# Last cross round rebuilt, the outer loop written out, and the low context made by adding transfers

## The reference

```python
x = _layernorm(x + attn(x))           # 4 "time" rows by 16 heads, and a dynamic convolution
x = _layernorm(x + xattn(x, ctx))     # this one:
    q  = (x @ w_q).reshape(b, n, 16, 64)
    kv = (context @ w_kv).reshape(b, 1601, 2, 16, 64)
    attn = softmax(einsum('bnhd,bmhd->bhnm', q, k) * 64 ** -0.5)
    out  = einsum('bhnm,bmhd->bnhd', attn, v) @ w_out + b_out
x = _layernorm(x + ffn(x))            # softmax over 8 gates, top 2, relu(x W1 + b1) W2 + b2
```

## Time and profile before

| | us |
|---|---|
| median of 3 runs | 1937.08 |
| lowest and highest | 1935.52, 1938.04 |
| profiled execution, its own time | 1938.37 |
| its span, first to last instruction | 1936.6 |

### The profile page before, as it was taken

One profiled execution on the slowest core, in us unless ns is written; L12 is line 12 of the kernel. 1 busy time (PEld: TensorE's weight loads), 2 busy tenths in 40 slices (PEclk: granted clock), 3 DMA queues, 4 the chain that ended last, 5 costly groups with the idle time before them and its releaser, 6 DMA issues. The chain is left out here.

```text
span 1936.6 us, 32752 instructions
## 1 busy us (share of the span) xinstructions
PE 1732.8 (89%) x10604; PEld 1207.0 (62%) x10604; DVE 1178.2 (61%) x2073; ACT 826.8 (43%) x1198; POOL 1277.1 (66%) x709
## 2 busy tenths in 40 slices
PE   6654699999989999998999999989999999847992
PEld 4543566666756666665666666757666665436991
DVE  4776455656565656666665556565656667666665
ACT  3223244444444444444544444444444445421223
POOL 3878248667686676776768577686776776933554
PEclk8776789999999999999999999999999999957996
DMA  6001300000200000010000000100000000241224
GB/s 196 1 22 33 120 1 23 1 23 0 78 1 23 1 24 15 9 56 23 23 1 23 2 23 0 63 16 23 1 23 15 8 16 12 84 145 49 75 77 144
DMA packets 39141, 71.24 MB, mean 37 GB/s; under 512 B 4632, under 2 KB 28568, under 8 KB 37728
## 3 DMA queue, kind: packets, MB, share of 16 engines
q1 hardware_dynamic: 35264, 59.27, 9.1%
q0 software_dynamic: 3744, 10.23, 1.7%
HBM read 55.97 MB, written 13.52 MB: 36 GB/s over the span
## 5 line engine op out<-in xcount | busy, mean ns | idle before, releaser
L1173 POOL TENSOR_TENSOR xa_total<-xa_total,xa_pexp 128x1024 f32<-128x1024 f32 (+1 forms) x341 | 832.4, 2441 | 59.7 <-ACT xa_pexp L1096 35.6
L1271 DVE TENSOR_REDUCE xa_parts<-ps_ring 128x1 f32<-128x402 f32 x1024 | 531.6, 565 | 268.5 <-PE ps_ring L1016 255.4
L1096 ACT ACTIVATE xa_pexp<-ps_s 128x1024 f32<-128x1024 f32 (+1 forms) x416 | 426.2, 1026 | 387.3 <-PE ps_s L970 349.6
L984 PE MATMUL ps_pv<-xa_pexp,xa_v 128*64 128x512 f32 (+1 forms) x1664 | 402.3, 607 | 0.0
L984 PEld LDWEIGHTS ps_pv<-xa_pexp,xa_v 128*64 128x64 f32 (+1 forms) x1664 | 106.7, 137 | 182.0 <-issue 141.6
L970 PE MATMUL ps_s<-xa_q_neg,xa_row_one 64*128 64x512 f32 (+1 forms) x832 | 180.8, 393 | 0.0
L1173 POOL TENSOR_TENSOR xa_total<-xa_pexp 128x1024 f32<-128x1024 f32 x31 | 74.0, 2386 | 159.8 <-ACT xa_pexp L1096 158.5
L1149 ACT COPY xa_v<-ps_ring 128x256 f32<-128x256 f32 (+1 forms) x208 | 77.5, 373 | 204.0 <-PE ps_ring L955 202.2
L1016 PE MATMUL ps_ring<-xa_k_hi,xa_q_hi 64*128 64x402 f32 x512 | 128.7, 378 | 7.8 <-DVE xa_parts L1271 6.9
L1016 PE MATMUL ps_ring<-first_k_hi,xa_q_hi 64*128 64x402 f32 x512 | 122.7, 386 | 3.3 <-DVE xa_q_lo L1265 1.5
L1326 DVE RECIPROCAL xa_inv<-xa_sums 128x128 f32<-128x128 f32 x124 | 116.9, 943 | 0.0
(11 more groups left out here) (303 smaller groups left out, 3376.9 us busy)
## 6 DMA issues: line engine op xcount, KB each, us to landing
wa_raw<-in_pack_a SPq DMA_DIRECT2D x17, 768.0 KB, 4.4
ex_raw<-in_pack_e SPq DMA_DIRECT2D x8, 1024.0 KB, 5.9
ctx_raw<-in_ctxT SPq DMA_DIRECT2D x4, 1601.0 KB, 8.8
wb_raw<-in_pack_b SPq DMA_DIRECT2D x16, 256.0 KB, 2.6
ex_w<-ybuf SPq DMA_DIRECT2D x8, 512.0 KB, 7.4
sa_xT<-in_xT SPq DMA_DIRECT2D x8, 256.0 KB, 6.3
X<-in_x SPq DMA_DIRECT2D x1, 2048.0 KB, 11.7
x_hi<-sa_x1s_hi SPq DMA_DIRECT2D x16, 128.0 KB, 2.1
```

Source lines behind the costliest of these rows:

```text
L984: ins = nc.tensor.matmul(ps_pv[half(h), :], v[0:m, t, at:at + XD], pexp[0:m, buf, h, :], start=t == 0, stop=t == MT - 1)
L1096: nc.scalar.activation(pexp[0:m, buf], ps_s[0:m, (p * MT + t) % 2], ACT.Exp, scale=XD ** -0.5)\
L1173: engine.tensor_tensor(total[p][0:m], first, pexp[0:m, buf], ALU.add).then_inc(s["add_done"], 1)
L1271: nc.vector.tensor_reduce(parts[:, h, q, c:c + 1], ps_ring[:, r, 0:CW], AX.X, ALU.max)\
```

## The change

- The loop over b is written out (three copies of its body); the loops over j stay.
- In a round that ends a batch, ScalarE copies the context halves behind tiles 4 and 6 (they were behind 5 and 8), and behind each copy (tiles 5 and 7) scales the high part by -1 into `ctx_lo` (CN). GpSimd then issues a transfer that adds `ctx_raw` to it. The subtractions of GpSimd and VectorE are gone.
- In the last round WX is split: ScalarE makes the high part, GpSimd the low one. Experts 1, 2 and 0, in that order, are made (the first two in the first half, tiles 3 and 5), expert 3 is left to the expert stage. In the first half the additions of tiles 9 to 12 are VectorE's. Two input buffers changed places in memory, so that the places of experts 1 and 2 are free early.
- In the expert stage experts 3, 4 and 5 have their low parts from GpSimd (5 behind the first gathers), the copy of 7 comes behind the fourth block, and the 32 comparisons of 128 elements are 4 of 1024 in float32.

```diff
@@ one_round
     if batch_ends:
-        loads = join(loads, {0: ([], [("LDC",)]), 2: ([], [("X1",)]), 5: ([], [("CX", 0)]), 8: ([], [("CX", 1)])})
+        loads = join(loads, {0: ([], [("LDC",)]), 2: ([], [("X1",)]), 4: ([], [("CX", 0)]), 5: ([], [("CN", 0)]), 6: ([], [("CX", 1)]), 7: ([], [("CN", 1)])})
...
-        loads = join(loads, {2 * b: ([], [("ST", b)]) for b in range(B - 1)})
+        loads = join(loads, {2 * b: ([], [("ST", b)]) for b in range(B - 1)}, {3: ([], [("WX", 0)]), 5: ([], [("WX", 1)])})
...
-        head = {0: ([], [("WX", 0)]), 1: ([], [("TX", 0), ("WX", 1)]), 3: ([], [("GT", 0), ("TX", 1)]), 5: ([], [("GT", 1), ("TX", 2)]),
-                6: ([], [("WX", 2)]), 7: ([], [("GT", 2), ("TX", 3), ("WX", 3)]), 9: ([], [("GT", 3), ("TX", 4)]),
+        head = {1: ([], [("TX", 0), ("WX", 2)]), 3: ([], [("GT", 0), ("TX", 1)]), 5: ([], [("GT", 1), ("TX", 2)]),
+                7: ([], [("GT", 2), ("TX", 3)]), 9: ([], [("GT", 3), ("TX", 4)]),
@@ walk
-    with eng.Fori(0, B - 1) as b:
+    for b in range(B - 1):
@@ Ahead
-EARLY = 4
+ORDER = (1, 2, 0, 3, 4, 5, 6, 7)
+EARLY = 3
@@ scalar, cross
+                elif kind == "WX":
+                    pos = st[1]
+                    act.wait_ge(ahead.raw_in[pos % STG], 16 * (pos // STG + 1))
...
+                    nc.scalar.copy(ahead.w_all[:, ORDER[pos], 0], ahead.raw[pos % STG][:]).then_inc(ah["w_hi_done"], 1)
...
+                elif kind == "CN":
+                    k = st[1]
+                    act.wait_ge(s["ctx_hi_done"], n.of("CX"))
+                    nc.scalar.mul(ctx_lo[:, k], ctx_hi[:, k].bitcast(F32), -1.0).then_inc(s["ctx_neg"], 1)
@@ additions
-        def adds_on_vector(i, p):
-
-            return isinstance(i, int) and i == QUADS * B - 1 and p == 1
+        def adds_on_vector(i, p, t):
+
+            return isinstance(i, int) and i == QUADS * B - 1 and (p == 1 or t >= 9)
@@ gpsimd, cross
-                elif kind == "CX" and st[1] == 0:
+                elif kind == "CN":
+
                     k = st[1]
-                    pool.wait_ge(s["ctx_hi_done"], n.of("CX") + 1)
-                    nc.gpsimd.tensor_tensor(ctx_lo[:, k], ctx_raw[:, k], ctx_hi[:, k].bitcast(F32), ALU.subtract)\
-                        .then_inc(s["ctx_lo_done"], 1)
+                    pool.wait_ge(s["ctx_neg"], n.of("CN") + 1)
+                    nc.gpsimd.dma_start(ctx_lo[:, k].bitcast(F32), ctx_raw[:, k], accum_op=ALU.add).then_inc(s["ctx_lo_done"], 16)
@@ vector, cross
-                elif kind == "CX" and st[1] == 1:
-
-                    dve.wait_ge(s["ctx_hi_done"], n.of("CX") + 1)
-                    nc.vector.tensor_tensor(ctx_lo[:, 1], ctx_raw[:, 1], ctx_hi[:, 1].bitcast(F32), ALU.subtract)\
-                        .then_inc(s["ctx_lo_done"], 1)
@@ experts
-            take_weights(6)
-            take_weights(7)
+            take_weights(5)
+            take_weights(6)
...
+                if q == 3:
+                    take_weights(7)
...
-                for k in range(n, n + 8):
-                    ins = nc.vector.tensor_scalar(one_r[:, k % 16], iota_h[:], rem[:, k:k + 1], None, ALU.is_equal)
-                ins.then_inc(s["one_r_done"], 1)
+                nc.vector.tensor_tensor(one_r[:, n % 16:n % 16 + 8], iota[:].unsqueeze(1).broadcast_to([P, 8, P]),
+                                        rem[:, n:n + 8].unsqueeze(2).broadcast_to([P, 8, P]), ALU.is_equal)\
+                    .then_inc(s["one_r_done"], 1)
```

More of the change, by code:

```diff
@@ L825, in start @@
         sp.dma_start(self.b1c[:], a["pack_e"][:, :, WW:].rearrange("e p c -> p e c")).then_inc(self.sems["small_in"], 16)
-        for e in range(STG):
-            self.load(sp, a, e)
+        for pos in range(STG):
+            self.load(sp, a, pos)
 def cross_attention(nc, a, X, consts, loads, first, ahead, x1_hi, x1_lo):
@@ L1183, in handle @@
                 if kind == "PV" and st[2] >= 1:
-                    if not adds_on_vector(i, st[1]):
+                    if not adds_on_vector(i, *st[1:]):
                         add(pool, nc.gpsimd, n, st)
@@ L1470, in _ @@
                 .then_inc(s["x2_out"], 16)
-            for e in range(STG + EARLY, NE):
-                lo_done(sp, e - STG + 1)
-                ahead.load(sp, a, e)
+            for pos in range(STG + EARLY, NE):
+                lo_done(sp, ORDER[pos - STG])
+                ahead.load(sp, a, pos)
             for r in range(3):
```

64 lines of the change are left out of this document (33 added, 31 removed).

## The result

The changed kernel takes 1908.32 us (median of 4 runs, 1906.95 to 1908.62) where the kernel before took 1937.56 beside it (4 runs). The ratio is 0.9843, 95% interval 0.9832 to 0.9855: by the ratio it is 30.4 us faster (29.2 by the two medians), with 28 to 33 inside the interval. The forecast was 1918.3, in a range of 1908 to 1930, a gain of 18.8. So the direction was right, but the gain is 1.6 times the forecast one: the time lies at the fast edge of the range, and the ratio times the 1937.08 from which the forecast started is 1906.7, just outside it. The profiled execution's span fell from 1936.6 to 1906.9 us, by 29.7.

A forecast was written before the change was run, and what follows sets the result against it. The prediction took TensorE to bound the cross rounds, so only its idle time could be gained. Its terms, -7.0 - 11.6 + 0.5 - 0.7 = -18.8 us, gave 1918.3 us, in a range of 1908 to 1930.

The forecast's parts named there:

- Part 1: Outer loop over b written out: two back edges and slower half rounds in the j loops go, -7.0 us.
- rival (d): Outer loop: fresh code is fetched as slowly as old code is jumped to, 5.7 us stay, 1924 us; chance 0.07.
- Part 2: Three batch ends, ctx_lo by scaling and adding transfers: 3.9 us each, -11.6 us, with ends of 19 and 9.
- Rival (b): Batch ends reach the plain 41.76 us (19.2 instead of 11.6) and GpSimd's additions run earlier: 1907 to 1911; chance 0.11.
- 11.8, so att_hi is ready at 31.3: Batch end: ScalarE's summed durations from the fourth exponential, 19.4 us in, put att_hi at 31.3 us into the half round.
- att_lo then takes 1.74 to 2.82 us: Batch end: VectorE's att_lo after att_hi takes 1.74 to 2.82 us, so the output projection starts at 33.2 to 34.3.
- the middle value of 44.3: Batch-end half round: 41.8 us plus 2.5 us of TensorE's wait beyond the plain round, 44.3 us.
- the ends of 4.6 and 15: Landing time of one 800 KB adding transfer, scaled by size from the nearest rows: 4.6 to 15 us; 9 us taken.
- rival (c): Batch ends: adding transfers in series at 15 us each stall TensorE at the next keys, +31.5 us, 1950; chance 0.08.
- Part 3: Last round: first half loses 15.7 us to VectorE's wait for addition 8, the rest gives 15.2 back, net +0.5 us.
- Rival (a): Last round does not give back what VectorE's wait for addition 8 costs: +8 us, 1926 us; chance 0.16.
- Part 4: Expert stage: four comparisons of 1024 elements replace 32 and a copy goes, -0.7 us; the extra weight costs nothing.

The follow-up runs named there:

- the subtraction moved: The kernel before, with VectorE's subtraction of the second half of ctx_lo given to GpSimd, no scaling or adding transfer: 1926.64 us, ratio 0.9926.
- the doses: The changed kernel, with the first 256 or 1280 elements of the second scaling done once more ahead of it: 1917.90 and 1923.38 us.
- the large dose: The changed kernel, with the first 1280 elements of the second scaling done once more ahead of it: 1923.38 us, ratio 0.9918.
- the kernel that lets VectorE by: The large dose, with GpSimd made to wait until att_lo is done before it issues the second adding transfer: 1911.80 us, ratio 0.9858.

## Why the prediction was right and where it was wrong

**Part 1 was right** to 0.1 us (-7.0) for the six half rounds it counted, in the changed kernel and alone; rival (d) falls. It left out the 21 others, which the written-out loop shortened by another 1.8 us.

**Part 2 held the mis-sized term:** 11.6 us forecast, 19.6 measured, nearly its own upper end of 19. Rival (b), at 0.11, was the case that came. Two steps of it failed, each with about half of the 2.5 us of wait that it took beyond a plain round.

The first is the sum over ScalarE's queue, "11.8, so att_hi is ready at 31.3". The durations were right, but adding them counts the overlap of 0.1 us between neighbours nine times, and the start was taken 0.3 us too late. 30.05 was measured; with it and the forecast's own lengths of att_lo the wait beyond a plain round would have been 0.6 to 1.8 us, not 1.9 to 3.0.

The second is "att_lo then takes 1.74 to 2.82 us", taken as a length with a range. It is 0.69 us of work and a wait for GpSimd. At the batch ends of ten kernels it ended 0.54 to 0.57 us behind the end of an addition wherever it came during one: 546.82 behind 546.28 here, 546.55 behind 545.99 with the subtraction moved. Both lengths that the forecast took from the earlier trace rows were such waits already. The old 2.82 us ended at 551.49 and the plain round's 1.74 us at 1459.60, behind GpSimd's additions that ended at 550.94 and 1459.06:

```profile
544.36 6.58 POOL L1173 TENSOR_TENSOR xa_total<-xa_total,xa_pexp 128x1024 f32<-128x1024 f32 x2
...
1456.35 2.71 POOL L1173 TENSOR_TENSOR xa_total<-xa_total,xa_pexp 128x1024 f32<-128x1024 f32 x1
```

So it is in every half round of the kernel before: all 31 of att_lo and all 31 of the product ahead of it (R2) in the cross rounds come during a GpSimd instruction and end 0.55 to 0.56 us behind it. In the changed kernel it is 30 of 31 for each; the odd one of each, in the last round's second half, came with GpSimd idle and took 0.69 us. The Trainium skill ("SBUF — State Buffer", section "SBUF: two separate sides") calls the pair of ports that these two engines share an exclusive lock: whichever starts first, a VectorE instruction with two SBUF inputs or a GpSimd one that reads SBUF, has it for its whole instruction and the other stands still. The traces agree, with the numbers above. The prediction named the contention for the last round, where it said that the additions would take 1.29 us each with GpSimd idle (1.22 and 1.29 were measured), and priced the batch end as if it were a slowdown.

So the middle value of 44.3 for the batch end lay where the kernel does not go: the doses show 41.5 to 41.8 or above 46. With att_hi at 31.35, the forecast's own time, the batch end takes 46.1 to 47.2 (the large dose), and part 2 would have given some 5 us, not 11.6. At two of its three batch ends the changed kernel is on the good side of the step by less than 0.46 us. At the forecast's own time of att_hi its lengths priced too little (44.3 against 46.1 to 47.2), and that time was 1.3 us too late, which decided on which side the kernel fell. So that the batch ends came out fully hidden, as rival (b) has it, hung on about half a microsecond that neither the forecast nor rival (b) had weighed: as a price it is luck.

That no wait for ctx_lo would come was right, by 6 to 7 us; the landing of 6.0 us lies between the ends of 4.6 and 15, and rival (c) falls. The prediction's estimate of 3.9 us by the Trainium skill ("DMA: Bandwidth & Descriptors", section "Anatomy of one DMA — SWDGE (gpsimd) path") was too low for these adding transfers: the measured 5.9 to 6.6 us decide.

**Part 3 was right** in the first half (61.0 us forecast and measured, by the same queue of addition 8, four maxima, three additions, negmax) and 1.5 us too careful in the second (52.9 against 51.4). Rival (a) falls. The net is nothing: the first half pays what the second gains, and the old last round itself differs by 2.5 us between four kernels.

**Part 4** came out at -1.3 instead of -0.7. The comparisons did as forecast, 5.28 to 4.62 us:

```profile
1716.64 4.62 DVE L1825 TENSOR_TENSOR ex_one_r<-ex_iota,ex_rem 128x1024 bf16<-128x1024 f32 x4
```

It was not tried by itself; the whole 1.3 us lies within what that stage differs between kernels that share it, so whether part 4 gained anything is not shown.

**The clock.** The old wait of 3.86 us had a row at 0.96. With the large dose TensorE waited 3.3 us at the first batch end, the row has 0.96, and the half round grew by 4.5; with the wait of 0.9 us in the kernel that lets VectorE by it is 1.00, and the half round grew by 0.9. With the same waits a row can read either way: the large dose's three batch ends waited 3.3 us each and read 0.96, 0.93 and 0.96 (46.3, 47.2 and 46.1 us), and the first half of the last round read 1.00 or 0.96, 1.6 us apart.

## What to carry to other kernels

Where VectorE has two SBUF inputs beside GpSimd, price neither a mean nor a range: find in the trace which GpSimd instruction runs when VectorE's comes, and take its end plus the length of VectorE's own instruction, less about 0.14 us (0.55 for one of 0.69, 1.08 for one of 1.22). A delay then costs nothing or one whole instruction of GpSimd, and where the critical path lies there, a wait that holds GpSimd back can be worth more than the idle time it makes (here 3.4 to 4.6 us for 2). Before a half round's change of 1 to 2 us is put down to an edit, compare the clock column of the two rows. Moving work in a list moves it in time only if the engine has something in front of it.
